# Expert inputs scaled on VectorE alone, weights prepared between the first groups, and a new order of work on all engines

## The reference

```python
x = x + linear_attention(ln_c(x))      # norm over channels, q/k/v by 128x128 weights, 8 heads of 16
t = to_tokens(x)
t = t + moe(ln_t(t))                   # norm over the 128 channels of a token
x = from_tokens(t)

# linear_attention: Q, K = elu(.) + 1; out_l = Q_l . (sum_{m<=l} K_m V_m^T) / (Q_l . sum_{m<=l} K_m)
# moe: logits = x @ gate_w + mean(ins @ rmod_w); probs = softmax; the two largest of 8 are kept
#      out = sum_e combine_e * (gam_e * (x @ expert_w_e + expert_b_e) + bet_e)
#      gam = mean(ins @ gamma_w.T), bet_e = ins-weighted rows of beta_w
```

## Time and profile before

| | us |
|---|---|
| median of 3 runs | 736.78 (733.86 to 740.26) |
| the profiled execution | 737.64 |
| its span, first to last instruction | 735.9 |
| TensorE busy | 681.8 (93%) |
| VectorE busy | 632.3 (86%) |
| GpSimd busy | 468.7 (64%) |
| ScalarE busy | 292.0 (40%) |

### The profile page before, as it was taken

How to read it: one execution, slowest core, us unless ns; L and a number is a source line. 1 busy time by engine, 2 the same in 40 slices (tenths; PEclk the granted TensorE clock), 3 DMA queues, 4 the chain that set the end, 5 groups by cost and what they waited for, 6 DMA issues and landing times.

```text
span 735.9 us, 35372 instructions
## 1 busy us (share of the span) xinstructions
PE 681.8 (93%) x13757; PEld 458.9 (62%) x13865; DVE 632.3 (86%) x1690; ACT 292.0 (40%) x865; POOL 468.7 (64%) x696
## 2 busy tenths in 40 slices
PE   3667999989999999999999999999999999999986
PEld 1656656656666666666666666666666666665542
DVE  3667999988999999999999999999999999988762
ACT  1134434433444444444444444444444444434311
POOL 5365765565667676767676767676767676764521
PEclk9788999999999999999999999999999999999997
DMA  4111111111111111111111111111111111011000
GB/s 109 53 35 32 45 32 46 46 45 32 45 43 43 43 43 43 43 43 43 43 43 42 44 42 43 42 44 42 44 42 43 42 43 41 29 31 33 17 17 29
DMA packets 60229, 30.53 MB, mean 41 GB/s; under 512 B 2160, under 2 KB 60176, under 8 KB 60176
## 3 DMA queue, kind: packets, MB, share of 16 engines
q1 hardware_dynamic: 60176, 29.79, 14.2%
HBM read 20.34 MB, written 9.44 MB: 40 GB/s over the span
## 4 chain that ended last, share of the span: by engine, by line
PE 82%; issue 8%; POOL 4%; DVE 4%; DMA 1%; ACT 1%; SPq 0%; DVEq 0%; POOLq 0%; ACTq 0%
PE bank_o L1134 31%; PE num L1048 7%; PE num L1031 5%; PE wide_a L1128 4%; PE wide_a L1000 3%; PE num L1015 3%; PE bank_g L1071 3%; PE bank_g L960 3%; PE bank_g L911 3%; PE bank_g L1086 2%; PE bank_g L975 2%; PE wide_a L943 2%; PE bank_o L1093 2%; PE wide_a L945 2%; PE wide_b L943 2%
## 5 line engine op out<-in xcount | busy, mean ns | idle before, releaser
L1134 PE MATMUL bank_o<-xs,e_w 128*128 128x512 f32 x576 | 279.7, 610 | 0.2 <-DVE xs L774 0.2
L1134 PEld LDWEIGHTS bank_o<-xs,e_w 128*128 128x128 f32 x576 | 99.3, 191 | 88.0 <-issue 87.5
L338 POOL TENSOR_TENSOR qn<-feat,rden 128x512 f32<-128x512 f32 x36 | 38.8, 1077 | 114.0 <-DVE rden L654 114.0
L374 POOL TENSOR_TENSOR xs<-spread,x 128x1024 f32<-128x1024 f32 x36 | 97.7, 2714 | 4.4 <-ACT spread L498 4.4
L774 DVE TENSOR_TENSOR xs<-wide_a,x 128x1024 f32<-128x1024 f32 x72 | 87.5, 1215 | 6.2 <-PE wide_b L1128 6.1
L456 ACT ACTIVATE q_eo<-bank_g,parity 128x512 f32<-128x512 f32 x72 | 45.5, 683 | 96.3 <-PE bank_g L975 96.3
L465 ACT ACTIVATE squares<-bank_g 128x128 f32<-128x128 f32 x108 | 28.5, 274 | 137.3 <-issue 70.0
L326 POOL TENSOR_TENSOR k_sum<-k_sum,feat 128x64 f32<-128x64 f32 x216 | 68.8, 318 | 16.9
L637 DVE SCALAR_TENSOR_TENSOR feat<-ex,qkv 128x512 f32<-128x512 f32 x72 | 79.3, 1103 | 0.0
L366 POOL TENSOR_TENSOR coef<-weight,coef 128x256 fp32r<-128x256 f32 x36 | 26.1, 724 | 83.0 <-ACT coef L486 83.0
L307 POOL TENSOR_TENSOR x_low<-x,x_high 128x512 fp32r<-128x512 f32 x36 | 61.1, 1697 | 4.6 <-ACT x_high L421 4.6
(11 more groups left out here) (161 smaller groups left out, 1630.7 us busy)
## 6 DMA issues: line engine op xcount, KB each, us to landing
x<-in_x SPq DMA_DIRECT2D x36, 256.0 KB, 2.9
x_res<-in_x SPq DMA_DIRECT2D x36, 256.0 KB, 2.9
out<-o SPq DMA_DIRECT2D x36, 256.0 KB, 2.5
beta_raw<-in_L_ffn_beta_w SPq DMA_DIRECT2D x1, 512.0 KB
e_raw<-in_L_ffn_expert_w SPq DMA_DIRECT2D x1, 512.0 KB
w_raw<-in_L_conv_Wkv SPq DMA_DIRECT2D x2, 64.0 KB, 2.4
b_qkv<-in_L_conv_bkv SPq DMA_DIRECT2D x1, 128.0 KB, 6.1
w_raw<-in_L_conv_Wq SPq DMA_DIRECT2D x1, 64.0 KB, 2.5
```

Source lines behind the costliest of these rows:

```text
L374: tt(xs[:, g.par, 2 * pair:2 * pair + 2], spread[:], flat(x1[:, g.par]).unsqueeze(1) .broadcast_to([128, 2, U * T]), ALU.mult).then_inc(S[ ...
L1134: last = mm(bank_o[:], e_w[:, e], xs[:, g.par, e], start=False, stop=(final and e % 2 == 1), skip_group_check=True)
```

## The change

**Scaling.** `spread_pair` on ScalarE, `scale_pair` on GpSimd and the buffer `spread` go. VectorE scales all four pairs from PSUM. `spread_scales(g, 0)` now comes first and serves pairs 0 and 1, `spread_scales(g, 1)` pairs 2 and 3:

```diff
@@ gpsimd
-            def scale_pair(g, pair, evac, done):
-                need(pool, evac, g.i + 1)
-                need(pool, "x1_done", g.i + 1)
-                need(pool, "out_done", g.i - 1)
-                tt(xs[:, g.par, 2 * pair:2 * pair + 2], spread[:], flat(x1[:, g.par]).unsqueeze(1)
-                   .broadcast_to([128, 2, U * T]), ALU.mult).then_inc(S[done], 1)
@@ scalar
-            def spread_pair(g, bank, scaled, done):
-                need(act, "spread1", g.i + 1)
-                need(act, scaled, g.i)
-                nc.scalar.activation(spread[:].rearrange("p n t -> p (n t)"), bank[:], copy).then_inc(S[done], 1)
@@ tensor, spread_scales (waits at the edges left out)
                 if k == 0:
-                    need(pe, "scaled2", g.i + 1)
-                    need(pe, "spread_evac", g.i + 1)
+                    need(pe, "prob0", g.i + 2)
+                    need(pe, "prob1", g.i + 2)
...
                 else:
-                    need(pe, "prob0", g.i + 2)
-                    need(pe, "prob1", g.i + 2)
+                    need(pe, "scaled0", g.i + 1)
+                    need(pe, "scaled1", g.i + 1)
+                    need(pe, "squares_done", g.i + 2)
+                    need(pe, "lg_done", g.i + 2)
```

```diff
+            def gammas_and_gate():
+                pe.wait_ge(S["consts"], CONSTS)
+                pe.wait_ge(S["rest_loaded"], 16 * REST_WEIGHTS)
...
+            def router():
+                pe.wait_ge(S["rest_dve"], GATE)
...
+            def expert_weights(half):
+                pe.wait_ge(S["rest_dve"], ROUTER + 4 * half)
+                mm(bank_o[:], centre[:], e_raw[:, 4 * half:4 * half + 4], start=True, stop=True).then_inc(S["rest_pe"], 1)
+
+            def expert_bias():
+                pe.wait_ge(S["rest_dve"], EXPERT_W)
...
+            def bias_rows():
+                pe.wait_ge(S["rest_dve"], BIASES)
```

```diff
@@ tensor, step
...
                 g = at(4)
                 if g:
+                    if first(g):
+                        expert_weights(0)
                     scores(g)
+                    from_state(g)
                 g = at(6)
                 if g:
-                    experts(g, 3, "scaled3", True)
+                    experts(g, 2, "scaled2", True)
...
-            first_weights()
-            rest_of_weights()
```

More of the change, by code:

```diff
@@ L177, in need, with first @@
                 eng.wait_ge(S[name], count)
+        def first(g):
+            return g.edge and g.i == 0
         def flat(v):
@@ L562, in first_weights @@
                     copy(mask32[rows], heads_mask[rows, rows]).then_inc(done, 1)
-                dve.wait_ge(S["first_pe"], 1)
-                copy(w_t[:], bank_g[:, 0:384]).then_inc(done, 1)
-                dve.wait_ge(S["first_loaded"], 16 * FIRST_WEIGHTS)
+                for b in range(PAR):
+                    nc.vector.memset(v_pad[:, b], 0.0).then_inc(done, 1)
+                nc.vector.memset(state[:], 0.0).then_inc(done, 1)
+                for n, at in ((0, EXPERTS), (0, 3 * EXPERTS), (1, ROWS + EXPERTS)):
+                    copy(place[:, n, at:at + EXPERTS], ident[0:EXPERTS, 0:EXPERTS]).then_inc(done, 1)
@@ new lines, in first_weights @@
+                for k in range(2):
+                    for part in range(2):
+                        at = 4 * k + 2 * EXPERTS * part
+                        nc.vector.reduce_sum(sel_parts[:, k, part:part + 1], ident[:, at:at + 3 * ROWS + 4:ROWS + 1],
+                                             axis=AX).then_inc(done, 1)
+                dve.wait_ge(done, 19)
+                nc.vector.reduce_sum(sel_rows[:], sel_parts[:], axis=AX).then_inc(done, 1)
+                dve.wait_ge(done, 20)
+                copy(sel[:], sel_rows[:].unsqueeze(2).broadcast_to([128, 2, 128])).then_inc(done, 1)
@@ L1153, in step @@
                 if g:
-                    experts(g, 0, "scaled0", False)
+                    experts(g, 3, "scaled3", False)
+                g = at(4)
+                if g:
+                    if first(g):
+                        expert_weights(0)
+                    scores(g)
+                    from_state(g)
+                g = at(6)
+                if g:
+                    experts(g, 2, "scaled2", True)
+                g = at(5)
+                if g:
+                    if first(g):
+                        bias_rows()
+                    coef_transposed(g)
+                g = at(4)
+                if g:
+                    if first(g):
+                        expert_weights(1)
+                    values(g)
+                g = at(5)
+                if g:
+                    spread_scales(g, 0, "spread0")
                 g = at(3)
                 if g:
+                    if first(g):
+                        gammas_and_gate()
+                    k_transposed(g)
                     key_values(g)
+                g = at(5)
+                if g:
+                    bias(g)
+                g = at(4)
+                if g:
+                    if first(g):
+                        expert_bias()
+                    x1_centred(g)
+                g = at(5)
+                if g:
+                    experts(g, 1, "scaled1", False)
+                    spread_scales(g, 1, "spread1")
                 g = at(0)
```

509 lines of the change are left out of this document (240 added, 269 removed).

## The result

The changed kernel takes 751.17 us (median of 4 runs, 750.21 to 752.51), the kernel before on the same chip 735.63: a ratio of 1.0203, interval 1.0151 to 1.0254. The forecast was 717.5 us, in a range of 701 to 735. The profiled execution spans 749.3 us against 735.9 before; the forecast made its span 716.9, so 32.4 us are to be explained.

What follows compares the result with a forecast made beforehand. It took TensorE, nearly gapless in the steady part, and a loop through TensorE and VectorE to bound the kernel. Span 735.9 - 13.8 + 6 - 6 - 6.2 + 1 = 716.9 us, giving 717.5 us, range 701 to 735.

Steps and rivals of the forecast that it cites:

- Part 1: Start: x transposed ahead of the other weights, so first statistics come at 13.6 us; -13.8 us.
- Part 2: Fill: other weights prepared between the groups' operations, half of their 12.2 us chain hidden in idle time; +6 us.
- Part 3: Shallower pipeline: from a group's statistics to its residual about half a step less, counted once; -6 us.
- Part 4: Early periods: VectorE's features no longer wait for GpSimd's scaling L374, four periods at 1.57 us each; -6.2 us.
- early excess: Six intervals between residuals from 88.76 us take 11.3 us more than six steady ones; 6.3 put down to features' waits.
- Part 5: Steady period: 18.41 us instead of 18.37, VectorE's added scaling hidden by its wait for TensorE; +1 us over 29 periods.
- The loop through both engines: Steady period: TensorE's values to spread, then VectorE's scaling to second causal product; longest of three sums, 18.4 us.
- A: Rival: the loop is looser and TensorE alone sets the steady period, 18.05 us or less; 706 us, chance 0.18.
- C: Rival: GpSimd's loop delays VectorE's denominators in the steady period, 1.3 us each; slower, 755 us, chance 0.09.
- Part 6: Loads and kernel end: counted at nothing; pair 3's scaling on VectorE at the end between -2 and +1 us.
- rival B: Start's gain given back: weights cost the whole 12.2 us and features still stalls; 730 us, chance 0.18.

Runs made afterwards that it cites:

- experiment 1: Changed kernel with its other weights prepared in one go ahead of group 0's statistics, not between the groups; 760.11 us, ratio 1.0362.
- the scaling alone: Kernel before with only pair 3's scaling moved to VectorE behind pair 2, order and weights as before; 743.18 us, ratio 1.0123.
- experiment 4: TensorE's loop three turns shorter, six more steps written out, in either kernel: changed kernel 753.95 us (1.0264), kernel before 742.92 us (1.0101).
- experiments 4 and 8: Experiment 4, and 8: loop's short wait list in full written-out steps; changed kernel 743.30 us; kernel before, with 112 empty weight loads too, 727.76 us.
- experiment 5: Changed kernel with from_state moved behind the two long expert products, so short products stand apart; 755.74 us, ratio 1.0283.
- half a block of padding: Changed kernel with 128 empty weight loads on TensorE between its loop and its written-out last steps; 744.43 us, ratio 1.0149.

## Why the prediction was wrong

By parts the 32.4 us are -1.6, +4.7, +8.6, +6.2, +2.8 and +11.4 (the drain's 11.7 less the 0.2 that the period adds there), and 0.3 of the tail and rounding. (The last step of the sum, 718.6 less 0.9, is 717.7 and not 717.5; that changes nothing.)

**Part 1, right.** First statistics at 12.04 us, forecast 13.6: 1.6 better. The runs with the same start and otherwise changed code have 13.0 to 13.2 in most, so half a microsecond is nearer.

**Part 2, mis-sized: +10.7 instead of +6** (experiment 1). I gave the engines' idle time in the fill as cover and took half. But each handshake is in program order on both engines, as the part itself said. The waits of the changed kernel from 20 to 75 us show the two longest:

```profile
DVE gamma_all L569 <- PE bank_o L891: 5.1, 1, 5.1
...
PE bank_o L896 <- DVE e_w L578: 2.1, 1, 2.1
```

Measured from the first statistics, the first values end 35.2 us later here and 26.2 with the weights ahead: 9.0 of the 10.7 are lost by then. The price near the upper bound was right to take. Up to 2.3 of the 10.7 may be no handshake: the chain of the changed kernel has a stop of 2.26 us ahead of a transpose at 26.40, 0.8 us behind a fetch that landed at 25.57, and with the weights ahead the same stop (2.32 us) is not on the chain:

```profile
24.14 2.26 issue
26.40 1.09 PE bank_g L921 x4
```

**Part 3, wrong in sign: +2.6 instead of -6.** Half a step less was counted in steps of equal length, not along a group's way. That way, without the weights, is as long as with the scaling alone up to the values (26.2 and 25.7 us from the first statistics); then the last scales of the router follow at 41.3 against 35.4, and 39.4 in the kernel before itself. In between x1_centred now stands behind a spread, key transposes, key-values and bias, and the router's operations share VectorE's order with four projections of another group. This reading of the difference is argued from the timelines, not tried. The same code's fill differs between executions by up to 2.6 us (73.2 to 75.8 in four of them), and the fill of before is 59.3 in the run of experiment 4, so the size is good to some 2 us; half a step is gained in none of them.

**Part 4, the lock right, its gain not seen.** No features operation between 86 and 210 us takes over 0.86 us (2.89 before; min, median and max in ns):

```profile
L622 DVE SCALAR_TENSOR_TENSOR feat<-ex,qkv x13: 627/787/854, 85.9 to 207.4; 128x512 f32<-128x512 f32 x13
```

Alone, the scaling saved 4.3 us there, with 2.4 of added period in the same six intervals, so 6.7 in all: near the 6.2. But the lock does not strike in every execution alike. In the run of experiment 4 on the kernel before, whose code is the same up to there, features wait for GpSimd in one of these periods (2.88 us, at 110.44) and not in four. The features of the kernel before, then of that run:

```profile
L637 DVE SCALAR_TENSOR_TENSOR feat<-ex,qkv x12: 675/1004/2892, 95.1 to 198.9; 128x512 f32<-128x512 f32 x12
```

```profile
L637 DVE SCALAR_TENSOR_TENSOR feat<-ex,qkv x13: 676/690/2881, 91.3 to 208.5; 128x512 f32<-128x512 f32 x13
```

Its six intervals take 118.16 us, 3.3 less for three locks less: 1.1 a lock, and 4.4 for four, an estimate from these two executions. Where the new order lost as much again in the same intervals is open. Its two fetch stops there (2.31 and 0.88 us, with one spell of half clock of 3.4 us behind the first) stand against two of 1.69 and 0.73 before, so they explain little of it. I had left the other half of the early excess unexplained; the longer waits of written-out steps were in it (experiments 4 and 8).

**Part 5, near: 18.53 instead of 18.41.** The loop through both engines did bind, as forecast; it is 0.1 longer, and with it loosened the period is still 18.33, 0.28 above the 18.05 worked out for TensorE. A change of tile shape, 0.25 in that sum, came to 0.16 in experiment 5; VectorE's idle time is 330.00 - 307.17 us over 18 periods, 1.27 each, and not the 0.6 of its sum. So that the wait for TensorE hides the added scaling was too kind: VectorE's 1.22 us cost 0.4 in the old order and some 0.2 in the new one. Rivals A and C fell: TensorE alone does not set the period, and the denominators hardly wait.

**Part 6, the step that failed most.** "At the end of the kernel between -2 and +1" was +11.7. I priced there what changes in the work, the scaling, and not where the code comes to lie. Of the 11.7, 5.4 are the three stops; with half a block of padding 10.7 go. What goes beyond the stops is the half clock in large part. The run with the weights ahead (experiment 1) has the same last steps and stops of 1.88, 2.40 and 1.52 us, but behind the first of them the clock stays at 2.4 GHz until the second (its windows view, columns as above):

```profile
683.90:703.00 19.10, 15.95 (x360) 9.74 (x363) 13.47 (x33) 5.54 (x20) 7.53 (x14) 1.00 0.11 31
```

Its drain is 107.96 us, 3.7 shorter, with TensorE busy for 94.24 us and not 98.36. The clock stands at half for 23.9 us of the changed kernel's drain, for 13.7 of this one and for 6.8 of before's (mean granted clock 0.89, 0.94 and 0.97). The 10.2 us less, beside 0.4 more of stops, give some 0.4 us for each us at half clock; by that price the 17.1 us more than before are 6.8, which with the 5.4 of stops is about the 11.7. This is an estimate from two executions, and why the clock fell behind one stop and not behind another was not found. The forecast's clock, stops and waits were taken as those of before, which had the same stops elsewhere (52.36 to 54.95 us) and which I had seen as "issue" without asking.

The Trainium skill (Runtime: NRT & Kernel Launch, Instruction fetch mechanics) says that code is refilled in blocks of 16 KiB, 256 instructions, the next while the current one runs, and that "the cost of crossing a 16 KiB boundary is one DMA tail-bump, mostly hidden". The block size agrees with the 768 and the 16 KB here; the "mostly hidden" holds for the blocks with long products here, and not for `values`, whose 256 instructions pass in 1.41 us, while a fetch takes 0.9 to 1.6 and TensorE goes on 1.2 to 1.5 us after it has landed.

By its mechanism rival B came nearest, the start given back (first residual 2.06 us earlier instead of 13.8), and its bound still missed the drain. By its number it was C, 755 against 751.17, and that was luck: the period that C needed, 1.3 us longer, was 0.16 longer.

## What to carry to other kernels

In code that is written out, find TensorE's idle time put down to "issue", and count its instructions between two stops: a multiple of 256 points to blocks of code that come late, and then an edit ahead of that place can move the time by a per cent, whatever else it does (128 empty loads took the median from 751.2 to 744.4 us here). Compare two orders of work only with that taken out, and a part of a run only with a second execution beside it. Weights that are prepared between groups are not hidden by idle time as such: they cost 10.7 us here, most of it where each handshake waits for its turn in both engines' order.

## Unexpected of the hardware

A run of 256 short instructions that fills one block stops TensorE for 1.4 to 2.4 us (1.4 to 2.1 in the changed kernel, where the granted clock then stood at half for 3.4 to 6.8 us; behind one such stop of another run it did not fall). 160 empty loads far ahead of a loop made it fetch code while it ran, and its 23 periods took 492.06 us instead of 426.09. And a VectorE operation of 32 elements that reads SBUF waited 2.1 us for a GpSimd one.
